# Loading the gate/up levels of the packed half tile once for both of its jobs, and one job earlier in the DMA queue for the jobs that follow

## The chip, the cores and the metric

The kernel runs on one NeuronCore of a Trainium2 chip. Its engines are TensorE (PE; its weight loads are PEld), VectorE (DVE), ScalarE (ACT), GpSimd (POOL) and SyncE (SP), which here only issues DMAs. The metric is device time in microseconds (us) of one execution. Before the change it is 1940.79 us, the median of 3 runs (1940.75 to 1940.89).

## The reference

One layer of a transformer-like tower on 16 x 128 tokens of 1024 features: a generated convolution kernel (the part called tok), then attention, then a gated feed-forward part with quantised weights. The change is in the feed-forward part:

```python
def _qlinear(x, q, scale, A, Bm):
    w = (q.astype(jnp.float32) - Q_ZERO) * (scale * Q_STEP)[:, None]
    y = jnp.einsum('bsh,oh->bso', x, w)
    return y + LR_SCALE * (x @ A @ Bm)
g = _qlinear(x, gate_q, gate_scale, gate_A, gate_B)     # q: (2752, 1024) integers 0..15
u = _qlinear(x, up_q, up_scale, up_A, up_B)
h = jax.nn.silu(g) * u
return _qlinear(h, down_q, down_scale, down_A, down_B)  # q: (1024, 2752)
```

Here x has 2048 rows of 1024 features, and 2752 is 21 tiles of 128 hidden features and a rest of 64.

## The kernel before, in words

**Jobs.** The gate and up products are done in 44 jobs. A job (i, p) is one tile i of hidden features for one half p of the tokens (two chunks, a and b, of 512 tokens each). The order is the list `JOBS`: jobs 0 and 1 are tiles 0 and 1 for the first half of the tokens, computed directly ("whole"). Jobs 2 and 3 are the packed half tile (i = 21) for the first and for the second half of the tokens: the 64 gate rows and the 64 up rows that are left over stand together in one tile of 128, so each of the two jobs has one product per chunk ("half"). Jobs 4 to 43 do tiles 2 to 20 for the first half of the tokens (jobs 4 to 22) and tiles 0 to 20 for the second (jobs 23 to 43), each with seven half-size products in place of eight ("seven"), in the manner of Strassen. Constants: `SEVENS` = 4 is the first of these, `SECOND` = 23 the first of the second half, `NJ` = 44, `FULL` = 21.

**What a job needs.** SP loads the job's integer levels into the one buffer `qraw` (q_raw in the trace: 1024 KB, 512 KB for the half tile), ACT converts them to 16-bit floats in `q16[g % 2]` (q_f in the trace; `convert`, L1671 to L1676), and for a job of seven products POOL forms four sums of them in `qsum[g % 2]` (q_sums; `level_sums`, L1097 to L1106). PE's first product of such a job uses q_f, the second uses q_sums. The semaphore `s_q` counts conversions. As `qraw` is one buffer, `load_rows` waits for the conversion of the load before:

```python
            sp.wait_ge(s_q, g)
```

**Behind the products.** DVE gathers the products of a job into gate and up, ACT applies silu and rounds the hidden values to 16 bits (`high_hidden`), POOL makes their rest (`low_hidden`, L1111, counted by `s_hlo`), and SP stores both (L1021, hidden_parts). PE adds the job's share of the low-rank product of down two jobs later (`inner_product`, L1404), after `s_hlo`. The semaphores of PE's steps on ACT's copies of the low-rank terms of gate and up (`s_term`) keep PE from writing ps_l before ACT has read it: job 4's first matmuls (L1386) wait for job 3's last such copy (`term_half`, first_up, L1716).

**The queue of SP** is written out by hand and every wait in it holds what stands behind it. At place g of its loop it does, in this order: `load_rows(g + 2)`; at g = 23 a load for down's low-rank part; from g = 23 on the load of one tile of down's integer levels (`load_levels`, L991, down_raw, 512 KB), and of two such tiles at g = 23 + 6, 23 + 12 and 23 + 18 (the tuple `TWICE`); the store of job g's hidden values, after `s_hlo`. down_raw is one buffer too, so `load_levels(i)` waits until POOL has converted tile i - 1 (`s_lev`).

**The loop of POOL** at place g: `low_hidden` of job g - 1, `level_sums(g + 1)`, and from g = 24 on the conversion of one tile of down's levels (`convert_levels`, L1115), of two tiles at g = 29, 35 and 41. There are 22 such tiles, 0 to 21: at place 29 POOL converts tiles 5 and 6. SP loads tile 5 at its place 28, and tiles 6 and 7 at its place 29.

**The loop of ACT** at place g: from g = 4 on it copies a low-rank term, applies silu and copies the first product, rounds the hidden values of job g - 1, and then does `convert(g + 1)`. For the jobs up to 4 it does `convert(g + 1)` at the start of the place.

**After the jobs**, down's products (L1511) run on PE.

Of the kernel before, what the change touches and what calls it, by code (L numbers as in the profile page):

```python
# [12 lines left out]
ACT = mybir.ActivationFunctionType  # L13
X = mybir.AxisListType.X

P = 128
# [518 lines left out]
KH = KT // 2  # L535
JOBS = [(0, 0), (1, 0), (FULL, 0), (FULL, 1)] + [(i, 0) for i in range(2, FULL)] + [(i, 1) for i in range(FULL)]
KINDS = ["half" if i == FULL else "whole" if g < 2 else "seven" for g, (i, _) in enumerate(JOBS)]
SEVENS = 4
SECOND = SEVENS + FULL - 2
TWICE = (6, 12, 18)  # L540
NJ = len(JOBS)


class Events:
# [18 lines left out]
PROD = Events(("a", "b"), ("gate_a", "up_a", "gate_b", "up_b"), ("p1", "p6", "p5", "p2", "p7", "p3", "p4"))  # L563
# [119 lines left out]
def layer(nc, t, out, first, rooms, small, xn_hi, xn_lo, ident, mask, h0_dram):  # L683
# [12 lines left out]
    two, four = range(2), range(4)  # L696
    w, wv, raw, raw_v, bias = first.w, first.wv, first.raw, first.raw_v, first.bias
# [43 lines left out]
    qraw = put("q_raw", [P, 2, D], I32, "w")  # L741
    q16 = [put(f"q_f16{s}", [P, 2, D], F16, "w", 8192 + 4096 * s) for s in two]
    qsum = [put(f"q_sums{s}", [P, 4, KH * P], F16, "v0", 8192 + 4096 * s) for s in two]
    hid = [put(f"hidden{s}", [P, BPP, 2, H], F16, "v0", 4096 * s) for s in two]
    q_zero = small("q_zero", [P, 1])
# [29 lines left out]
    with ExitStack() as st:  # L775
# [18 lines left out]
    s_qraw, s_q, s_qsum, s_lraw, s_lev = (sem("g_" + n) for n in ("qraw", "q", "qsum", "lraw", "lev"))  # L794
    s_prod, s_low, s_term, s_first, s_read, s_silu, s_hid, s_hhi, s_hlo, s_inner = (
        sem("g_" + n) for n in ("prod", "low", "term", "first", "read", "silu", "hid", "hhi", "hlo", "inner"))
# [42 lines left out]
    def _(sp):  # L839
# [133 lines left out]
                spread_low(n // 4 - 1)  # L973
        def load_rows(g):
            i = JOBS[g][0]
            sp.wait_ge(s_q, g)
            if i < FULL:
                sp.dma_start(qraw[:], t["gu_q"][i, :, :, :]).then_inc(s_qraw, 16)
            else:
                sp.dma_start(qraw[:, 0, :], t["gu_q"][i, :, 0, :]).then_inc(s_qraw, 16)  # L980
# [11 lines left out]

        level = 0
        for g, (i, p) in enumerate(JOBS):
            if 0 < g < NJ - 2:
                load_rows(g + 2)
            if g == SECOND:
                sp.wait_ge(s_prod, PROD.end(SECOND - 1))
                for done in (s_t1l, s_t3l, s_e2):
                    sp.wait_ge(done, 2 * KH)  # L1000
                sp.dma_start(bd_raw[:], t["down_b"]).then_inc(s_bdraw, 16)
            if g >= SECOND:
                for _ in range(2 if g - SECOND in TWICE else 1):
                    if level < IT:
                        load_levels(level)
                        level += 1
            if g == SECOND + 6:
                sp.wait_ge(s_bd, 1)
                sp.wait_ge(s_t2l, 2 * KH)
                for k in two:  # L1010
                    sp.wait_ge(s_out[k], 16 * (SECOND // 2 + (1 - k) * (SECOND % 2)))
                load_parts(0)
            sp.wait_ge(s_hlo, 2 * g + 2)
            rows = slice(p * BPP, (p + 1) * BPP)
            if i < FULL:
                dst = hid_dram[rows, :, i * 2 * P:(i + 1) * 2 * P].rearrange("n p f -> p n f")
                src = hid[g % 2][:].rearrange("p n a t -> p n (a t)")
            else:
                dst = hid_dram[rows, :, i * 2 * P:HB].rearrange("n p f -> p n f")
                src = hid[g % 2][:, :, 0, :]  # L1020
            sp.dma_start(dst, src).then_inc(s_out[g % 2], 16)  # L1021
# [25 lines left out]
    def _(pool):  # L1047
# [48 lines left out]

        def level_sums(g):  # L1097

            gate1, gate2, up1, up2 = (q16[g % 2][:, m, at * KH * P:(at + 1) * KH * P] for m in two for at in two)
            sum1, sum2, sum3, sum4 = (qsum[g % 2][:, k, :] for k in four)  # L1100
            pool.wait_ge(s_q, g + 1)
            pool.wait_ge(s_prod, PROD.end(g - 2))
            chain.after(tt(sum1, up1, up2, ALU.add))
            chain.after(tt(sum2, sum1, gate1, ALU.subtract))
            chain.mark(tt(sum3, gate1, up1, ALU.subtract))
            tt(sum4, gate2, sum2, ALU.subtract).then_inc(s_qsum, 1)  # L1106
# [23 lines left out]
        for g in range(NJ):  # L1130
# [9 lines left out]
            if SEVENS <= g < SEVENS + 4 * KH:  # L1140
                p, k = sum_at(g)
# [20 lines left out]
    def _(pe):  # L1162
# [202 lines left out]
        def all_features(g, m, bank, p, c):  # L1365

            free(g, bank)
            for k in range(KT):
                lev = q16[g % 2][:, m, k * P:(k + 1) * P]
                nc.tensor.matmul(banks[bank], lev, x2_hi[:, k, chunk(p, c)], start=(k == 0), stop=False)  # L1370
                last = nc.tensor.matmul(banks[bank], lev, x2_lo[:, k, chunk(p, c)], start=False, stop=(k == KT - 1))
            last.then_inc(s_prod, 1)
# [52 lines left out]
        pe.wait_ge(s_term, TERM(0, "up_a"))  # L1425
        low(0, 1, 1, 1)
        for g in (1,):
            pe.wait_ge(s_q, g + 1)
            all_features(g, 0, 0, 0, 0)
            pe.wait_ge(s_term, TERM(g - 1, "gate_b"))  # L1430
            low(g, 0, 0, 0)
            all_features(g, 1, 1, 0, 0)
            pe.wait_ge(s_term, TERM(g - 1, "up_b"))
            low(g, 1, 0, 1)
            all_features(g, 0, 2, 0, 1)
            pe.wait_ge(s_term, TERM(g, "gate_a"))
            low(g, 0, 1, 0)
            all_features(g, 1, 3, 0, 1)
            pe.wait_ge(s_term, TERM(g, "up_a"))
            low(g, 1, 1, 1)  # L1440
        for g in (2, 3):
            p = JOBS[g][1]
            pe.wait_ge(s_q, g + 1)
            all_features(g, 0, 0, p, 0)
            for c in two:
                pe.wait_ge(s_lst[2 * p + c], 16 * 16)
            pe.wait_ge(s_term, TERM(g - 1, "gate_b" if g == 2 else "a"))
            low_half(g, 0)
            inner_product(g - 2)
            all_features(g, 0, 2, p, 1)  # L1450
            pe.wait_ge(s_term, TERM(g - 1, "up_b" if g == 2 else "b"))
            low_half(g, 1)
        for g in range(SEVENS, NJ):
            p = JOBS[g][1]
            a, b, side = chunk(p, 0), chunk(p, 1), 1 + 2 * (g % 2)
            q, sums, fresh = q16[g % 2], qsum[g % 2], g in (SEVENS, SECOND)
            one, two_ = slice(0, KH), slice(KH, KT)
            left, right = slice(0, KH * P), slice(KH * P, D)
            pe.wait_ge(s_q, g + 1)
            if g == SEVENS:  # L1460
                pe.wait_ge(s_term, TERM(g - 1, "b"))
            else:
                pe.wait_ge(s_read, READ(g - 1, "w2"))
            low(g, 0, 0, 0)
            low(g, 0, 1, 1)
            free(g, 0)
            half_features(0, q[:, 0, left], x2_hi[:, one, a], x2_lo[:, one, a], False)
            inner_product(g - 2)
            pe.wait_ge(s_qsum, g - SEVENS + 1)
            if fresh:  # L1470
                pe.wait_ge(s_t2l, KH * (p + 1))
            free(g, side)
            half_features(side, sums[:, 1, :], x2_hi[:, one, b], x2_lo[:, one, b], False)
            pe.wait_ge(s_term, TERM(g, "gate_a"))
            low(g, 1, 1, 0)
            if fresh:
                pe.wait_ge(s_t1l, KH * (p + 1))
            free(g, 2)
            half_features(2, sums[:, 0, :], t1[p][0], t1[p][1], False)
            pe.wait_ge(s_first, SNAP(g, "up"))  # L1480
            half_features(0, q[:, 0, right], x2_hi[:, two_, a], x2_lo[:, two_, a], True)
            pe.wait_ge(s_read, READ(g, "w1"))
            low(g, 1, 0, 1)
            if fresh:
                pe.wait_ge(s_t3l, KH * (p + 1))
            pe.wait_ge(s_read, READ(g, "v"))
            half_features(side, sums[:, 2, :], t3[p][0], t3[p][1], True)
            pe.wait_ge(s_read, READ(g, "x5"))
            half_features(2, sums[:, 3, :], x2_hi[:, two_, b], x2_lo[:, two_, b], True)
            if fresh:  # L1490
                pe.wait_ge(s_t4l, KH * (p + 1))
            pe.wait_ge(s_read, READ(g, "x7"))
            half_features(side, q[:, 1, right], t4[p][0], t4[p][1], True)
# [48 lines left out]
    def _(act):  # L1542
# [126 lines left out]
            nc.scalar.activation(bst[:, m, :], b_raw[:], ACT.Copy, scale=ups[:, 1 + m:2 + m]).then_inc(s_bhi, 1)  # L1669

        def convert(g):  # L1671
            act.wait_ge(s_qraw, 16 * (g + 1))
            if g >= 2:
                act.wait_ge(s_prod, PROD.end(g - 2))
            m = slice(0, 2 if JOBS[g][0] < FULL else 1)
            nc.scalar.activation(q16[g % 2][:, m, :], qraw[:, m, :], ACT.Identity, bias=q_zero[:]).then_inc(s_q, 1)  # L1676

        deviation(0)
        high_features(0)
# [86 lines left out]
            high_sum(0, k, e1[0][k][:], t1[0][0][:, k, :], s_t1h, s_e1)  # L1766
        for g in range(NJ):
            kind = KINDS[g]
            if 2 <= g + 1 <= SEVENS:
                convert(g + 1)  # L1770
            if g == SEVENS - 1:
                act.wait_ge(s_prod, PROD.end(2))
                for k in range(KH):
# [16 lines left out]
            if g:  # L1790
                high_hidden(g - 1, 1)
                high_hidden(g - 1, 0)
            if SEVENS < g + 1 < NJ:
                convert(g + 1)
            if kind == "whole":
                term(g, 0, 1, 0)
# [579 lines left out]
```

## Time and profile before

| | before |
|---|---|
| time, median of 3 | 1940.79 us |
| the profiled execution: its time | 1940.61 us |
| its span (first to last instruction) | 1938.8 us |
| PE busy | 1813.0 us, 94% of the span |
| DVE busy | 1201.4 us, 62% |
| POOL busy | 860.2 us, 44% |
| ACT busy | 714.1 us, 37% |
| mean granted TensorE clock | 0.989 of full speed |
| mean DMA traffic | 101 GB/s |

The jobs run from about 1023 us to about 1630 us of the span, down's products after that. Busy is the share of time in which an engine has an instruction under way. The rows in the section below are of two kinds: in a timeline row the columns are start in us, duration in us (of several merged instructions together where it ends in x2, x3, ...), engine, source line, operation, output and inputs, and in brackets the idle time of the engine just before and what ended it.

### The profile page before, as it was taken

The page shows a single profiled execution, that of the slowest core. Times are in us where ns is not written, and L with a number is a line of the kernel's source. Part 1 is how long each engine was busy: PE and PEld are TensorE (multiplying, and loading weights), DVE is VectorE, ACT ScalarE, POOL GpSimd, SP SyncE. Part 2 cuts the span into 40 slices and gives each one's busy share as a digit, 9 for nine tenths or more (in the row PEclk, how much of TensorE's full clock was granted, in tenths as well). Part 3 has the DMA queues.
Part 4 walks back from the last instruction along what each step waited for, and adds up shares of the span by engine and source line. Part 5 has one row for each costly group of instructions (what it writes and reads, how often), then busy time and mean ns, then how long its engine had stood idle before and what let it go on. Part 6 is the DMA issues. An engine that isn't in the chain of part 4 may idle for free.

```text
span 1938.8 us, 31415 instructions
## 1 busy us (share of the span) xinstructions
PE 1813.0 (94%) x12892; PEld 990.2 (51%) x12892; DVE 1201.4 (62%) x1570; ACT 714.1 (37%) x1027; POOL 860.2 (44%) x593
## 2 busy tenths in 40 slices
PE   0586999999999999999999899999999999999999
PEld 0586665656666656545554344444444444444444
DVE  8996577787878888855657677775755554111111
ACT  4478243343433344422114454453544443000000
POOL 6973134343333334432361576665677774010111
PEclk9988999999999999999999899999999999999999
DMA  2122211111112211144531333434455544434341
GB/s 97 44 66 67 62 56 22 34 39 41 52 53 78 80 60 61 66 158 167 165 104 55 120 109 120 130 99 141 142 181 177 171 155 153 153 102 153 107 148 44
DMA packets 102847, 195.44 MB, mean 101 GB/s; under 512 B 14320, under 2 KB 75504, under 8 KB 92208
## 3 DMA queue, kind: packets, MB, share of 16 engines
q1 hardware_dynamic: 102704, 193.43, 31.2%
q8 instruction: 103, 1.69, 0.4%
q14 instruction: 40, 0.33, 0.1%
HBM read 136.24 MB, written 56.11 MB: 99 GB/s over the span
## 4 chain that ended last, share of the span: by engine, by line
PE 75%; DVE 9%; POOL 2%; issue 2%; ACT 2%; DMA 1%; DVEq 0%; SPq 0%; ACTq 0%
PE acc L1511 15%; PE acc L1377 12%; PE acc L1379 12%; PE ps_p L1169 4%; PE ps_p L1171 4%; PE ps_p L1170 4%; PE acc L1283 3%; PE acc L1285 3%; PE acc L1284 3%; PE ps_t L1196 3%; PE ps_p L1185 2%; PE ps_p L1186 2%; PE ps_p L1187 2%; PE ps_l L1386 2%; POOL prob L1058 1%
## 5 line engine op out<-in xcount | busy, mean ns | idle before, releaser
L1058 POOL TENSOR_TENSOR prob<-prob,mx 128x1024 f32<-128x1024 f32 x64 | 121.4, 1896 | 371.0 <-DVE mx L1878 371.0
L1169 PE MATMUL ps_p<-x_hi,w_qk 128*128 128x512 f16 x512 | 194.7, 380 | 0.0
L1170 PE MATMUL ps_p<-x_lo,w_qk 128*128 128x512 f16 x512 | 194.0, 379 | 0.0
L1171 PE MATMUL ps_p<-x_hi,w_qk 128*128 128x512 f16 x512 | 194.0, 379 | 0.0
L2265 DVE TENSOR_TENSOR y<-acc,down_scale 128x1024 f32<-128x1024 f32 (+1 forms) x17 | 19.8, 1162 | 252.8 <-PE acc L1511 252.8
L1111 POOL TENSOR_TENSOR hidden<-up,hidden 128x512 f16<-128x512 f32 x80 | 91.1, 1160 | 143.0 <-ACT hidden L1737 142.8
L1159 POOL TENSOR_TENSOR lr_term<-lr_term,h_again 128x1024 f32<-128x1024 f32 x16 | 37.6, 2348 | 253.6 <-ACT lr_term L1825 253.6
L1185 PE MATMUL ps_p<-w_v,x_hi 128*128 128x256 f16 x512 | 140.7, 275 | 3.7 <-PEq L805 3.6
L1063 POOL TENSOR_TENSOR prob<-prob,sm 128x1024 f32<-128x1024 f32 x64 | 120.1, 1896 | 52.9 <-DVE sm L1885 52.9
L1186 PE MATMUL ps_p<-w_v,x_hi 128*128 128x256 f16 x512 | 140.7, 275 | 0.0
L1187 PE MATMUL ps_p<-w_v,x_lo 128*128 128x256 f16 x512 | 140.6, 275 | 0.0
L1571 ACT ACTIVATE pth<-ps_t 128x512 f16<-128x512 f32 x128 | 76.1, 595 | 163.8 <-PE ps_t L1196 163.7
L258 PE MATMUL ssm_ps<-phase,magnitude 128*128 128x128 f32 x512 | 70.7, 298 | 64.9 <-DVE magnitude L469 61.7
L2130 DVE SCALAR_TENSOR_TENSOR up<-acc,gu_scale,up 128x512 f32<-128x512 f32 x120 | 90.0, 750 | 61.1 <-PE acc L1379 60.0
L2130 DVE SCALAR_TENSOR_TENSOR gate<-acc,gu_scale,gate 128x512 f32<-128x512 f32 x120 | 89.7, 748 | 56.1 <-PE acc L1379 55.3
L1377 PE MATMUL acc<-x_hi,q_f 128*128 128x512 f16 x320 | 122.3, 382 | 0.0
L1379 PE MATMUL acc<-x_lo,q_f 128*128 128x512 f16 x320 | 122.2, 382 | 0.0
L1377 PE MATMUL acc<-x_hi,q_sums 128*128 128x512 f16 x320 | 121.7, 380 | 0.0
L1379 PE MATMUL acc<-x_lo,q_sums 128*128 128x512 f16 x320 | 121.3, 379 | 0.0
L1377 PE MATMUL acc<-x_sum,q_sums 128*128 128x512 f16 x320 | 121.3, 379 | 0.0
L1379 PE MATMUL acc<-x_sum,q_sums 128*128 128x512 f16 x320 | 121.3, 379 | 0.0
L1889 DVE SCALAR_TENSOR_TENSOR ptl<-ps_t,pth 128x512 f16<-128x512 f32 x128 | 87.7, 685 | 47.2 <-ACT pth L1571 46.8
(343 smaller groups left out, 4382.6 us busy)
## 6 DMA issues: line engine op xcount, KB each, us to landing
q_raw<-in_gu_q SPq DMA_DIRECT2D x42, 1024.0 KB, 6.2
hid_parts<-hidden_parts SPq DMA_DIRECT2D x16, 1376.0 KB, 6.6
hidden_parts<-hidden SPq DMA_DIRECT2D x42, 512.0 KB, 3.5
down_raw<-in_down_q SPq DMA_DIRECT2D x22, 512.0 KB, 3.7
w_raw<-in_w_qk SPq DMA_DIRECT2D x8, 1024.0 KB, 4.9
h_tokens<-n_tok SPq DMA_DIRECT2D x16, 512.0 KB, 3.7
o_parts<-ot SPq DMA_DIRECT2D x32, 256.0 KB, 2.3
wv_raw<-in_w_o SPq DMA_DIRECT2D x8, 1024.0 KB, 4.8
```

Source lines behind the costliest of these rows:

```text
L1058: nc.gpsimd.tensor_tensor(prob[s % 2][p][:], prob[s % 2][p][:], bc(mx[p][:], H, 2), ALU.subtract).then_inc(s_sub[p], 1)
L1063: nc.gpsimd.tensor_tensor(prob[s % 2][p][:], prob[s % 2][p][:], bc(sm[p][:], H, 2), ALU.mult).then_inc(s_prob[p], 1)
L1169: nc.tensor.matmul(out[:], w[:, j % 2, m, 0, at], xn_hi[:, k, tok], start=(k == 0), stop=False)
L1170: nc.tensor.matmul(out[:], w[:, j % 2, m, 0, at], xn_lo[:, k, tok], start=False, stop=False)
L1171: last = nc.tensor.matmul(out[:], w[:, j % 2, m, 1, at], xn_hi[:, k, tok], start=False, stop=(k == KT - 1))
L1185: nc.tensor.matmul(out, xn_hi[:, k, tok], wv[:, g % 2, 0, at], start=(k == 0), stop=False)
L1186: nc.tensor.matmul(out, xn_hi[:, k, tok], wv[:, g % 2, 1, at], start=False, stop=False)
L1187: last = nc.tensor.matmul(out, xn_lo[:, k, tok], wv[:, g % 2, 0, at], start=False, stop=(k == KT - 1))
L1377: nc.tensor.matmul(banks[bank], lev[:, k * P:(k + 1) * P], hi[:, k, :], start=(k == 0 and not adds), stop=False, skip_group_check=adds)
L1379: last = nc.tensor.matmul(banks[bank], lev[:, k * P:(k + 1) * P], lo[:, k, :], start=False, stop=(k == KH - 1), skip_group_check=adds)
L1511: last = nc.tensor.matmul(acc[n % 2][:, b, :], parts[n % 3][:, at], levels[i][:, b * CH:(b + 1) * CH], start=(i == 0 and part == 0), stop= ...
L2130: stt(to[:], banks[bank], scl[:, m, i:i + 1], to[:], ALU.mult, ALU.add).then_inc(s_read, 1)
```

## The change

The two jobs of the packed half tile use the same levels. They are now loaded once and converted once, into one of the two buffers q_f, and both jobs read them there. `LOADS[g]` gives the number of the load whose levels job g uses (0, 1, 2, 2, 3, 4, ..., 42), and takes the place of g in the choice of the buffer and in the counts waited for. The loads of jobs 4 and later are issued one place earlier in SP's loop: `load_rows(4)` and `load_rows(5)` at places 0 and 1, `load_rows(g + 3)` at places 3 to 40. ACT converts job 4's levels where it converted job 3's.

```diff
+LOADS = [g if g < SEVENS - 1 else g - 1 for g in range(NJ)]
...
         def load_rows(g):
             i = JOBS[g][0]
-            sp.wait_ge(s_q, g)
+            sp.wait_ge(s_q, LOADS[g])
...
         for g, (i, p) in enumerate(JOBS):
-            if 0 < g < NJ - 2:
-                load_rows(g + 2)
+            if g < 2:
+                load_rows(g + SEVENS)
+            if 2 < g < NJ - 3:
+                load_rows(g + 3)
...
         def level_sums(g):
-            gate1, gate2, up1, up2 = (q16[g % 2][:, m, at * KH * P:(at + 1) * KH * P] for m in two for at in two)
+            gate1, gate2, up1, up2 = (q16[LOADS[g] % 2][:, m, at * KH * P:(at + 1) * KH * P] for m in two for at in two)
...
-            pool.wait_ge(s_q, g + 1)
+            pool.wait_ge(s_q, LOADS[g] + 1)
...
         def convert(g):
-            act.wait_ge(s_qraw, 16 * (g + 1))
+            act.wait_ge(s_qraw, 16 * (LOADS[g] + 1))
             if g >= 2:
-                act.wait_ge(s_prod, PROD.end(g - 2))
+                act.wait_ge(s_prod, PROD.end(1 if g == SEVENS else g - 2))
             m = slice(0, 2 if JOBS[g][0] < FULL else 1)
-            nc.scalar.activation(q16[g % 2][:, m, :], qraw[:, m, :], ACT.Identity, bias=q_zero[:]).then_inc(s_q, 1)
+            nc.scalar.activation(q16[LOADS[g] % 2][:, m, :], qraw[:, m, :], ACT.Identity, bias=q_zero[:]).then_inc(s_q, 1)
...
-            if 2 <= g + 1 <= SEVENS:
-                convert(g + 1)
+            if g == 1:
+                convert(2)
+            if g == 2:
+                convert(SEVENS)
```

PE's waits on `s_q` and its choice of q16 change in the same way, to `LOADS[g] + 1` and `LOADS[g] % 2`.

**SP where the half tile's jobs are.** Before, the rows of SP's queue from the store of job 0 on (hidden0 and hidden1 are the buffers of hidden values; a row of 128x1024 into q_raw is the half tile; the wait is named by its semaphore, g_q being `s_q` and g_hlo `s_hlo`):

```order
L1021 DMA hidden_parts<-hidden0_1975 128x8x256 [waits g_hlo]
L980 DMA q_raw_1970<-in_gu_q 128x1024 [waits g_q]
L1021 DMA hidden_parts<-hidden1_1976 128x8x256 [waits g_hlo]
L978 DMA q_raw_1970<-in_gu_q 128x2048 [waits g_q]
L1021 DMA hidden_parts<-hidden0_1975 128x8x128 [waits g_hlo]
```

The same stretch now:

```order
L979 DMA q_raw_1970<-in_gu_q 128x2048 [waits g_q]
L1024 DMA hidden_parts<-hidden0_1975 128x8x256 [waits g_hlo]
L979 DMA q_raw_1970<-in_gu_q 128x2048 [waits g_q]
L1024 DMA hidden_parts<-hidden1_1976 128x8x256 [waits g_hlo]
L1024 DMA hidden_parts<-hidden0_1975 128x8x128 [waits g_hlo]
```

The second load of the half tile is gone, job 4's load stands before the store of job 0 (it stood behind the store of job 1), and job 5's before the store of job 1.

**ACT where job 4's levels are converted.** Before (q_f160 and q_f161 are the two buffers of converted levels; x_hi and sum belong to the operands of the seven products):

```order
L1676 ACTIVATE q_f161_1972<-q_raw_1970,q_zero_1977 128x1024
L1716 ACTIVATE first_gate_1964<-ps_l,g_half_back_1952 128x512
L1729 ACTIVATE gate11_1959<-gate11_1959 128x512
L1737 ACTIVATE hidden1_1976<-up11_1963 128x4x128
L1737 ACTIVATE hidden1_1976<-up10_1962 128x4x128
L1716 ACTIVATE first_up_1965<-ps_l,g_half_back_1952 128x512
L1729 ACTIVATE gate00_1956<-gate00_1956 64x512
L1676 ACTIVATE q_f160_1971<-q_raw_1970,q_zero_1977 128x2048
L1744 ACTIVATE x_hi_64<-sum200_2006 128x512
```

And now:

```order
L1679 ACTIVATE q_f161_1972<-q_raw_1970,q_zero_1977 128x2048
L1719 ACTIVATE first_gate_1964<-ps_l,g_half_back_1952 128x512
L1732 ACTIVATE gate11_1959<-gate11_1959 128x512
L1740 ACTIVATE hidden1_1976<-up11_1963 128x4x128
L1740 ACTIVATE hidden1_1976<-up10_1962 128x4x128
L1719 ACTIVATE first_up_1965<-ps_l,g_half_back_1952 128x512
L1732 ACTIVATE gate00_1956<-gate00_1956 64x512
L1747 ACTIVATE x_hi_64<-sum200_2006 128x512
```

The full conversion stands where the half one stood, and the place where it stood is closed up.

**SP where down's levels are loaded twice** (places 28 and 29). Before, from the store of job 27 on:

```order
L1021 DMA hidden_parts<-hidden1_1976 128x8x256 [waits g_hlo]
L978 DMA q_raw_1970<-in_gu_q 128x2048 [waits g_q]
L991 DMA down_raw_2023<-in_down_q 128x1024 [waits g_lev]
L1021 DMA hidden_parts<-hidden0_1975 128x8x256 [waits g_hlo]
L978 DMA q_raw_1970<-in_gu_q 128x2048 [waits g_q]
L991 DMA down_raw_2023<-in_down_q 128x1024 [waits g_lev] x2
```

And now:

```order
L1024 DMA hidden_parts<-hidden1_1976 128x8x256 [waits g_hlo]
L979 DMA q_raw_1970<-in_gu_q 128x2048 [waits g_q]
L992 DMA down_raw_2023<-in_down_q 128x1024 [waits g_lev]
L1024 DMA hidden_parts<-hidden0_1975 128x8x256 [waits g_hlo]
L979 DMA q_raw_1970<-in_gu_q 128x2048 [waits g_q]
L992 DMA down_raw_2023<-in_down_q 128x1024 [waits g_lev] x2
```

The rows read alike; what differs is the job whose levels are loaded and the count that the load waits for. At place 29 it was job 31's load, behind the conversion of job 30's levels; it is job 32's load, behind the conversion of job 31's.

## Rows read from the trace of the kernel before

**Rows 1.** Windows: us, busy us of each engine, clock, DMA share, GB/s

```profile
1152.00:1330.00 178.00, 178.00 (x839) 77.58 (x838) 123.91 (x162) 85.67 (x117) 119.15 (x101) 1.00 0.37 116
```

**Rows 2.** Waits from 1000 to 1130 us: total us, times, longest us

```profile
PE ps_l L1386 <- ACT first_up L1716: 8.9, 1, 8.9
...
ACT q_f L1676 <- DMA q_raw<-in_gu_q: 7.7, 1, 7.7
```

**Rows 3.** Timeline of SP's queue around the half tile's jobs

```profile
1048.60 1.24 SPq L949 DMA_DIRECT2D low_stack<-low_lo  x2
...
1067.06 0.58 SPq L978 DMA_DIRECT2D q_raw<-in_gu_q  x1
```

**Rows 4.** Timeline of ACT, same stretch

```profile
1060.30 1.13 ACT L1676 ACTIVATE q_f<-q_raw,q_zero 128x1024 f16<-128x1024 int32 x1
...
1073.28 2.00 ACT L1676 ACTIVATE q_f<-q_raw,q_zero 128x2048 f16<-128x2048 int32 x1 [7.67 <-DMA q_raw<-in_gu_q]
...
1077.83 0.61 ACT L1729 ACTIVATE gate<-gate 64x512 f32<-64x512 f32 x1
...
1081.79 0.67 ACT L1716 ACTIVATE first_up<-ps_l,g_half_back 128x512 f32<-128x512 f32 x1
```

**Rows 5.** Timeline of PE, jobs 3 and 4

```profile
1068.98 0.41 PE L1391 MATMUL ps_l<-low_stack,gu_b_stack 128*64 128x512 f16 x2
...
1073.31 0.41 PE L1391 MATMUL ps_l<-low_stack,gu_b_stack 128*64 128x512 f16 x2
1082.60 1.01 PE L1386 MATMUL ps_l<-low_stack,gu_b_stack 128*128 128x512 f16 x2 [8.88 <-ACT first_up L1716]
...
1087.25 0.39 PE L1377 MATMUL acc<-x_hi,q_sums 128*128 128x512 f16 x1
...
1096.65 0.38 PE L1377 MATMUL acc<-x_sum,q_f 128*128 128x512 f16 x1 [0.17 <-DVE up L2130]
```

**Rows 6.** Timeline of DVE, same stretch

```profile
1062.56 1.30 DVE L2136 TENSOR_TENSOR up<-gate,up 128x512 f32<-128x512 f32 x2 [2.03 <-ACT gate L1729]
...
1078.48 2.74 DVE L2136 TENSOR_TENSOR up<-gate,up 64x512 f32<-64x512 f32 x2 [10.30 <-ACT gate L1729]
...
1087.44 0.76 DVE L2113 SCALAR_TENSOR_TENSOR up<-acc,g_half_scl,first_up 64x512 f32<-64x512 f32 x1
```

**Rows 7.** A window of PE's wait, columns as in Rows 1

```profile
1077.00:1078.00 1.00, 0.00 (x0) 0.00 (x0) 0.00 (x0) 1.00 (x3) 0.92 (x2) 0.50 0.00 0
```

**Rows 8.** Timeline of ACT: conversions of levels of jobs 30 and 31

```profile
1429.33 2.00 ACT L1676 ACTIVATE q_f<-q_raw,q_zero 128x2048 f16<-128x2048 int32 x1
...
1442.93 2.00 ACT L1676 ACTIVATE q_f<-q_raw,q_zero 128x2048 f16<-128x2048 int32 x1
```

**Rows 9.** Timeline of SP's queue, place 29

```profile
1431.79 0.58 SPq L978 DMA_DIRECT2D q_raw<-in_gu_q  x1
1439.02 6.89 SPq L991 DMA_DIRECT2D down_raw<-in_down_q  x2
```

**Rows 10.** Timeline of POOL: level tile 6, last sum for job 31

```profile
1442.78 2.77 POOL L1115 TENSOR_SCALAR x_hi<-down_raw 128x1024 f16<-128x1024 int32 x1 [3.79 <-DMA down_raw<-in_down_q]
...
1451.44 1.15 POOL L1106 TENSOR_TENSOR q_sums<-q_f,q_sums 128x512 f16<-128x512 f16 x1
```

**Rows 11.** Timeline of PE: start of job 31, its second product

```profile
1451.99 0.59 PE L1386 MATMUL ps_l<-low_stack,gu_b_stack 128*128 128x512 f16 x2
...
1454.80 0.39 PE L1377 MATMUL acc<-x_hi,q_sums 128*128 128x512 f16 x1
```

**Rows 12.** Source line L991: the 22 loads of down's levels

```profile
DMA to landing us min/median/max: 3.4/3.7/7.4
```

**Rows 13.** Source line L978: the 40 full loads of gate/up levels

```profile
DMA to landing us min/median/max: 4.8/6.2/9.9
```

**Rows 14.** Timeline of POOL: level tiles 13 and 20

```profile
1524.36 2.77 POOL L1115 TENSOR_SCALAR x_lo<-down_raw 128x1024 f16<-128x1024 int32 x1 [3.72 <-DMA down_raw<-in_down_q]
...
1606.67 2.77 POOL L1115 TENSOR_SCALAR down_levels<-down_raw 128x1024 f16<-128x1024 int32 x1 [4.39 <-DMA down_raw<-in_down_q]
```

More of the change, by code:

```diff
@@ L1368, in all_features @@
             for k in range(KT):
-                lev = q16[g % 2][:, m, k * P:(k + 1) * P]
+                lev = q16[LOADS[g] % 2][:, m, k * P:(k + 1) * P]
                 nc.tensor.matmul(banks[bank], lev, x2_hi[:, k, chunk(p, c)], start=(k == 0), stop=False)
@@ L1427, in _ @@
         for g in (1,):
-            pe.wait_ge(s_q, g + 1)
+            pe.wait_ge(s_q, LOADS[g] + 1)
             all_features(g, 0, 0, 0, 0)
@@ L1442, in _ @@
             p = JOBS[g][1]
-            pe.wait_ge(s_q, g + 1)
+            pe.wait_ge(s_q, LOADS[g] + 1)
             all_features(g, 0, 0, p, 0)
@@ L1455, in _ @@
             a, b, side = chunk(p, 0), chunk(p, 1), 1 + 2 * (g % 2)
-            q, sums, fresh = q16[g % 2], qsum[g % 2], g in (SEVENS, SECOND)
+            q, sums, fresh = q16[LOADS[g] % 2], qsum[g % 2], g in (SEVENS, SECOND)
             one, two_ = slice(0, KH), slice(KH, KT)
             left, right = slice(0, KH * P), slice(KH * P, D)
-            pe.wait_ge(s_q, g + 1)
+            pe.wait_ge(s_q, LOADS[g] + 1)
             if g == SEVENS:
@@ L1792, in _ @@
                 high_hidden(g - 1, 0)
-            if SEVENS < g + 1 < NJ:
+            if SEVENS <= g < NJ - 1:
                 convert(g + 1)
```

## The prediction

> **What bounds the kernel now.** I read the windows first, then the waits, then the timelines around the longest wait of TensorE, and last the timelines further on of every queue that the change touches. In the jobs of seven products PE is busy for all of 178 us, at full clock, while every other engine has spare time [rows 1]: what is added elsewhere costs nothing there until it makes PE wait. The largest wait of PE in the feed-forward part is one of 8.9 us, and ACT waits 7.7 us for a load of levels [rows 2]. The timelines join the two. SP has issued its last low_stack copies by 1048.60 + 1.24 = 1049.84 us, but job 4's load goes out only at 1067.06 [rows 3]. ACT has it at 1073.28 after 7.67 us of idling, converts for 2.00 us, and only then reaches first_up at 1081.79, on which PE has been waiting since the end of job 3 [rows 4, 5]. The wait has a second price, the clock: in the middle of it the granted clock is 0.50, the 1.2 GHz level, against 1.00, the 2.4 GHz level, in the steady jobs [rows 1, 7]. From the start of job 4 to its second product PE takes 1087.25 - 1082.60 = 4.65 us, and 1454.80 - 1451.99 = 2.81 us for the same piece of job 31 at full clock [rows 5, 11].
>
> **The change, part by part: the early gain.** Job 4's load is issued behind the low_stack copies, at 1049.9 us, since the conversion that it waits for is long done. With the usual 6.2 us to landing it is there at 1056.1, with the longest, 9.9, at 1059.8 [rows 13]: both ahead of ACT's turn at 1060.30. That conversion is now the full one, 2.00 for 1.13 us [rows 4], and it pushes what follows it on ACT, and through it DVE and PE in job 3, by 0.87 us. The half conversion of job 3 and one 512 KB load go; their time lay in the waits. PE then ends job 3 at 1073.31 + 0.41 + 0.87 = 1074.59 [rows 5]. ACT's other work need not be late: its copy of job 3's first term can start at 1068.98 + 0.41 + 0.87 = 1070.26, the silu some 0.67 us later, at 1070.9, and DVE's product 0.65 us behind that (1077.83 to 1078.48), at 1071.55 [rows 4 to 6]; the rounding of job 2's hidden values follows within 2 us. So what is late next is PE's own last matmul of job 3: first_up starts at 1074.6 and job 4 0.81 us behind it (1081.79 to 1082.60), at 1075.4. That is 7.2 us early, with an idle time of 0.8 us that I take as too short to cost clock. By its second product PE would be 1087.25 - (1075.4 + 2.81) = 9.0 us early. But at the end of job 4 PE waits for DVE even now, 0.17 us [rows 5], so it cannot gain more than DVE does. DVE's chain runs without a pause from 1078.48 to the L2113 at 1087.44; its first two products took 2.74 us there and 1.30 at 1062.56 [rows 6]. From 1071.55, with 1.30 for 2.74, it reaches L2113 at 1079.07 instead of 1087.44: 8.4 us early. I take -8.4. The bounds: -7.0, if the slow pair of DVE's products comes again (1.44 us), and -9.0, PE's own figure. POOL's sums for job 4 start earlier, within its idle time.
>
> **The part that costs: SP's waits further on.** From place 3 on, each `load_rows` stands at the same spot in the queue, but loads a job further, and so waits for one conversion more. qraw is one buffer, so that wait is needed. Conversions come every 13.6 us [rows 8]; the load at place g used to find its conversion done, and now waits nearly a whole job for it, with everything behind it. Behind it stand the store of hidden values and, from place 23, down's levels.
>
> The stores first. Before, the store of job g is released by POOL's low_hidden; the conversion of job g + 2's levels ends at about the same time, so the store is later by one issue, 0.6 us. Its readers (the buffer's next use two jobs later) are 20 us off: nothing.
>
> The single level tiles: a tile that was issued some 7 us behind low_hidden is now issued 0.6 us behind the end T of the next conversion. POOL must wait for it until T + 6.6; its 2.77 us end at T + 9.4, and low_hidden is due again some 2.3 us (an estimate) before the next conversion ends, at T + 11.3. That fits, also with a landing of 7.4 us (T + 10.8). Nothing.
>
> The double tiles at places 29 and 35 do not fit. POOL there converts tile 5, and then tile 6, which SP issues in its place 29. Now it is issued at 1439.02, as soon as POOL has freed the buffer; the 6.89 us of the row are the distance to the second of the two [rows 9]. POOL gets it at 1442.78 after a wait of 3.79 us, and then needs until 1451.44 + 1.15 = 1452.59 for the tile, low_hidden and the sums of job 31: 9.81 us [rows 10]. PE takes these sums at 1454.80 [rows 11], so the slack is 2.2 us. After the change the load in front of tile 6 waits for the conversion of job 31's levels, which ends at 1442.93 + 2.00 = 1444.93 [rows 8]. It takes 0.58 us to issue, so tile 6 goes out at 1445.55, behind 1024 KB. No row shows a level tile right behind such a load alone. Bounds: 3.8 us from issue to POOL's start, as now, and 7.4, the longest of the 22 [rows 12]. A 1024 KB load with a 512 KB store just in front takes 6.2 [rows 13], and a tile behind 1024 KB waits for the same 1536 KB; I take 6.0. POOL starts at 1451.55, the sums are done at 1461.4, and PE, which has nothing else to do, stands still for 6.6 us (4.3 to 8.0 by the bounds). At the end of the long wait of today the clock was at the lower level, and the restart cost 4.65 - 2.81 = 1.8 us. I take this again, since the stall is of that kind; bounds 0 and twice it, 3.6. Place 35 has the same distances [rows 14], where POOL waits 3.72 us for tile 13 as it waits 3.79 us for tile 6 at place 29. Two stalls: 2 x (6.6 + 1.8) = 16.8 us.
>
> Two sentences bear on this, and no number above needs them. The Trainium skill, page "DMA: Bandwidth & Descriptors", section "Anatomy of one DMA — SWDGE (gpsimd) path", says that DMA engines do not wait on semaphores, the wait is done by the issuing sequencer before dispatch. By that rule tile 6 cannot pass the load ahead of it, and the rival of no stall is excluded; the trace agrees in that SP issues nothing between 1431.79 and 1439.02. The same section of the Trainium skill fits a DMA with a fixed 2.0 us plus its bytes at 436 GB/s, for another way of issuing; the estimate by it for 1.5 MB is 5.6 us from the load's issue, 5.0 from the tile's, and the sum would be 2 us lower.
>
> The double tile at place 41 has no `load_rows` in front (they end at place 40), only tile 19 is late. The conversion at place 40 ends at 1442.93 + 2.00 + 11 x 13.6 = 1594.5; tile 19 is issued at 1595.1, there at 1601.1, converted at 1603.9; tile 20 follows 4.4 us later (POOL's wait of today) [rows 14], at 1608.3, and the sums end at 1618.1, where PE wants them at 1454.80 + 12 x 13.6 = 1618.0. So +0.1, up to 1.5 us with a landing of 7.4.
>
> **The sum.** -8.4 + 16.8 + 0.1 = +8.5 us. The profiled execution took 1940.6 us (span 1938.8 and 1.8 around it), the median of the runs is 1940.8, 0.2 more. So 1940.8 + 8.5 = 1949.3 us, 0.4% slower. Of this kernel a measurement tells about 0.2%, 3.9 us, from no change.
>
> **The rivals.**
> - *No stall, faster.* The early gain is real, and down's levels are never waited for. It decides itself at places 29 and 35: POOL would have to start on tile 6 by 1444.8 us (slack 2.2 us behind 1442.78). Against it: the issue alone is at 1445.55. For it: only that I may have the counts of the wait or the order of the queue wrong. Time: 1940.8 - 8.4 = 1932.4 us.
> - *Short stalls, no change.* The tile lands as fast as it does now, and the clock does not fall, since low_hidden done at mid-stall lets PE do its small inner product and cuts the idle time in two. 2 x 4.3 - 8.4 = +0.2: 1941.0 us. For it: most level tiles take 3.7 us; against it: 1024 KB are in front.
> - *Longer stalls.* The tile takes 9.9 us, as the slowest load of levels did [rows 13], behind the stores and loads that now bunch up: 2 x (10.5 + 1.8) - 8.4 + 1.5 = +17.7: 1958.5 us.
>
> **How the numbers follow.** Forecast 0.80, no stall 0.10, short stalls 0.06, longer stalls 0.04. The forecast's own range, from -9.0 with stalls of 4.3 and little clock to -7.0 with 8.0 and a bit over 1.8, is about 1943 to 1956; it, and short stalls at its edge, hold somewhat over 8 in 10, and the range stops there, with the fast case left out. Of the forecast's 0.80 I put 0.01 below 1944.7. Faster 0.10, within 0.2% 0.07, slower 0.83.
>
> **What the profile after would show.** Job 4's conversion at about 1060.3 us with no wait for its DMA, and job 4's first matmul at about 1075.4; PE then some 8.4 us early up to job 30. Then two waits of PE for q_sums of POOL in jobs 31 and 37, each of 4 to 8 us (in part before the inner product), with a clock of 0.5 at its end, and POOL waiting some 11 us for down_raw at places 29 and 35 where it waited 3.8. I am wrong if SP issues tile 6 before the conversion of job 31 ends, if PE shows no wait after 1400 us, or if its wait before job 4 is not shorter than 3 us. Wrong in size only, if the tile's landing or the clock's share differ.

## The result, and the profile after

| | before | after |
|---|---|---|
| time, median of 4 runs each | 1940.77 us | 1955.39 us |
| lowest and highest | 1939.27, 1940.89 | 1954.16, 1957.09 |
| the profiled execution: its time, its span | 1940.61, 1938.8 us | 1956.57, 1954.8 us |
| mean granted TensorE clock | 0.989 | 0.985 |

The changed kernel is slower: 1.0078 of the time before, 95% interval 1.006 to 1.0095. The forecast was 1949.3 us, within 1943 to 1956. The direction was right, and so was the mechanism of the stalls; of the +14.6 us the forecast had +8.5, and most of what is missing lies in its early gain.

The waits of PE over 0.8 us between 1000 and 1660 us of the changed kernel (total us, times, longest us):

```profile
PE acc L1380 <- POOL q_sums L1109: 9.7, 2, 4.8
PE ps_i L1407 <- POOL hidden L1114: 3.8, 2, 1.9
PE acc L1373 <- DVE up L2118: 3.4, 1, 3.4
PE ps_l L1389 <- ACT first_up L1719: 0.9, 1, 0.9
```

The wait of 8.9 us of [rows 2] has become 0.9 (last row). Two waits of 4.8 us for POOL's sums are new, each with one of 1.9 in front of it, and a wait that was 1.5 us before is now 3.4 (third row); of that one the forecast has only 0.87 us, for the longer conversion, and nothing for the clock.

SP's queue in the changed kernel, around the half tile's jobs and at place 29, which answer to [rows 3, 9]:

```profile
1052.84 0.58 SPq L979 DMA_DIRECT2D q_raw<-in_gu_q  x1
1056.04 0.38 SPq L1024 DMA_DIRECT2D hidden_parts<-hidden  x1
1065.27 0.34 SPq L979 DMA_DIRECT2D q_raw<-in_gu_q  x1
...
1443.30 0.33 SPq L979 DMA_DIRECT2D q_raw<-in_gu_q  x1
1443.67 8.84 SPq L992 DMA_DIRECT2D down_raw<-in_down_q  x2
```

Job 4's load goes out at 1052.84 instead of 1067.06, although this execution was 2.97 us late by then (see the table below). The load in front of tile 6 waits for the conversion of job 31's levels, 1441.28 + 2.00 = 1443.28 on ACT, and leaves 0.02 us later; tile 6 follows at 1443.67. ACT's conversion for job 4, which answers to [rows 4], has lost its wait of 7.67 us for the load:

```profile
1063.26 1.99 ACT L1679 ACTIVATE q_f<-q_raw,q_zero 128x2048 f16<-128x2048 int32 x1
```

What POOL and PE make of tile 6, timelines of the changed kernel that answer to [rows 10, 11]:

```profile
1449.38 2.77 POOL L1118 TENSOR_SCALAR x_hi<-down_raw 128x1024 f16<-128x1024 int32 x1 [9.88 <-DMA down_raw<-in_down_q]
...
1458.36 1.60 POOL L1109 TENSOR_TENSOR q_sums<-q_f,q_sums 128x512 f16<-128x512 f16 x1
```

```profile
1450.33 0.59 PE L1389 MATMUL ps_l<-low_stack,gu_b_stack 128*128 128x512 f16 x2
...
1454.55 0.62 PE L1407 MATMUL ps_i<-hidden,down_a 128*64 128x512 f16 x4 [1.89 <-POOL hidden L1114]
...
1460.01 0.61 PE L1380 MATMUL acc<-x_hi,q_sums 128*128 128x512 f16 x1 [4.84 <-POOL q_sums L1109]
...
1466.20 0.38 PE L1380 MATMUL acc<-x_hi,q_f 128*128 128x512 f16 x1
```

POOL waits 9.88 us for tile 6 where it waited 3.79; its last sum ends at 1459.96, and PE's second product starts at 1460.01. Undisturbed it would start 2.81 us behind 1450.33, at 1453.14: PE stands still for 6.87 us. The lower clock adds to it. Windows of the changed kernel (columns as in [rows 1]):

```profile
1459.00:1460.00 1.00, 0.00 (x0) 0.00 (x0) 0.61 (x1) 1.00 (x2) 0.95 (x1) 0.50 0.96 289
...
1464.00:1465.00 1.00, 1.00 (x4) 0.30 (x2) 1.00 (x2) 0.00 (x0) 1.00 (x2) 0.50 1.02 434
...
1466.00:1467.00 1.00, 1.00 (x6) 0.47 (x5) 0.60 (x1) 0.00 (x0) 0.92 (x2) 1.00 0.75 288
```

The granted clock is at the 1.2 GHz level at the end of PE's stall and for some 5 us more of work, and back at 2.4 GHz by 1466.

**Where the time is, piece by piece.** PE's timeline gives the start of each job (its first pair of low-rank matmuls, L1386 before, L1389 after). The table compares the profiled execution of every kernel with that of before. "Start" is where the pair in job 1 begins, 1039.82 us before; "early" is the time from there to the start of job 5, 58.56 us before (42.78 to job 4, and job 4's 15.78); then jobs 31 and 37, 13.61 us each before. Everything is in us, as the difference to before. The kernels e1 to e6 are those of the experiments below.

| kernel | start | early | job 31 | job 37 | sum | its time less 1940.61 |
|---|---|---|---|---|---|---|
| after | +2.97 | -4.63 | +9.38 | +8.26 | +15.98 | +15.96 |
| e1_levels_first | -2.17 | -4.58 | 0 | 0 | -6.75 | -6.76 |
| e2_one_double_fewer | -0.03 | -5.86 | 0 | +8.92 | +3.03 | +3.01 |
| e3_before_tile_held | -0.95 | -0.08 | +7.36 | +7.20 | +13.53 | +13.55 |
| e4_sums_held | +0.66 | -3.47 | +8.65 | +9.63 | +15.47 | +15.46 |
| e5_late_conversion | +0.18 | -8.03 | 0 | 0 | -7.85 | -7.89 |
| e6_two_loads_early | +1.42 | -5.88 | 0 | 0 | -4.46 | -4.48 |

The last two columns agree within 0.04 us in every kernel, so nothing else moved. The column "start" is not the edit's: none of the kernels changes an instruction ahead of that point. In the changed kernel the difference arises in the first 160 us. This is the window of 0 to 160 us, before and then after:

```profile
0.00:160.00 160.00, 80.63 (x618) 78.94 (x619) 142.69 (x153) 94.87 (x170) 122.52 (x107) 0.95 0.21 66
```

```profile
0.00:160.00 160.00, 78.57 (x591) 76.71 (x592) 145.81 (x150) 92.19 (x165) 118.08 (x105) 0.94 0.21 66
```

PE shows 27 matmuls fewer by then; from 160 to 1000 us its busy time is 808.59 us before and 808.53 after. The start differs by up to 5 us between executions. Without it the change costs -4.63 + 9.38 + 8.26 = +13.0 us in the profiled executions.

### The profile page after: what moved, and what is told of

It is laid out like the page before. It is cut to its first block, busy times and chain, and to the rows that moved or that the text cites. A ratio compares the mean times of both kernels' runs of the same rounds, so it can differ in the third digit from the quotient of the medians.

```text
span 1954.8 us, 31412 instructions
## 1 busy us (share of the span) xinstructions
PE 1819.0 (93%) x12892; PEld 992.3 (51%) x12892; DVE 1211.4 (62%) x1570; ACT 713.4 (36%) x1026; POOL 860.3 (44%) x593
## 4 chain that ended last, share of the span: by engine, by line
PE 72%; DVE 9%; POOL 3%; issue 3%; ACT 2%; DMA 1%; SPq 0%; DVEq 0%; ACTq 0%; POOLq 0%
PE acc L1514 15%; PE acc L1380 11%; PE acc L1382 11%; PE ps_p L1172 4%; PE ps_p L1174 4%; PE ps_p L1173 4%; PE acc L1286 3%; PE acc L1288 3%; PE acc L1287 3%; PE ps_t L1199 3%; PE ps_p L1188 2%; PE ps_p L1189 2%; PE ps_p L1190 2%; PE ps_l L1389 2%; POOL prob L1061 1%
```

## The experiments

The theory: the stalls of jobs 31 and 37 come from one thing, tile 6 (and 13) standing behind a load that waits for a conversion; and nearly half of the early gain was lost because POOL's sums for job 4 ran beside DVE's products. A rival for the first is that the bunched traffic itself slows the tiles; for the second, that the fall of the clock has nothing to do with POOL. The first rival did not hold up; for the second e4 and e5 speak.

**e1_levels_first.** From place 23 on the level tiles go ahead of the load in SP's queue.

```diff
-            if 2 < g < NJ - 3:
+            if 2 < g < SECOND:
                 load_rows(g + 3)
...
                         load_levels(level)
                         level += 1
+            if SECOND <= g < NJ - 3:
+                load_rows(g + 3)
```

> After, but from place 23 on SP issues down's level tiles of a place before the load of gate/up levels of that place. My theory (the wait in front of the tile in SP's queue makes the two stalls): tile 6 goes out as soon as POOL has freed its buffer, jobs 31 and 37 take 13.6 us each again instead of 23.0 and 21.9, and the time is that of before less the early gain of 4.6 us, 1936 us. The rival (the tile is late because more DMA traffic now bunches up around it): it lands late from wherever it is issued, POOL still waits over 6 us for it, and at least half of the 17.6 us stays, 1945 us or more.

Measured: 1933.95 us (median of 6; before on the same chip 1940.39), 0.9967 of before, interval 0.9954 to 0.998. SP's queue and POOL at place 29, timelines of e1_levels_first:

```profile
1432.28 6.84 SPq L992 DMA_DIRECT2D down_raw<-in_down_q  x2
1439.16 0.43 SPq L979 DMA_DIRECT2D q_raw<-in_gu_q  x1
```

```profile
1435.99 2.77 POOL L1120 TENSOR_SCALAR x_hi<-down_raw 128x1024 f16<-128x1024 int32 x1 [3.74 <-DMA down_raw<-in_down_q]
```

POOL's wait is the 3.7 us of before, both jobs are back at 13.61, and PE has no wait for q_sums. The waits of PE that are left here:

```profile
PE acc L1375 <- DVE up L2120: 3.4, 1, 3.4
PE ps_l L1391 <- ACT first_up L1721: 0.9, 1, 0.9
```

The order in the queue is the whole loss of jobs 31 and 37, and the early gain is as small as in the changed kernel.

**e2_one_double_fewer.** The changed kernel with `TWICE = (12, 18)` for `(6, 12, 18)`: place 29 converts one tile.

> After, with double level tiles at places 35 and 41 only (21 tiles are converted by place 43, and the 22nd as well: 20 places and two doubles). My theory: each double tile with a load in front makes one stall, so job 31 takes 13.6 us and only job 37 about 22 us; 9.4 us less than after, 1946 us in a run like its median. The rival (the stalls belong to these two jobs, by buffers or counts of conversions, not to the double tiles): both jobs stay long, 1955 us.

Measured: 1943.62 us (one run). Only job 37 is long, and PE waits for the sums once:

```profile
PE acc L1380 <- POOL q_sums L1109: 4.8, 1, 4.8
```

So the stall needs the double tile: a single one fits behind the late load, as the prediction has it. The time is 2.4 us under the expected 1946, in part by the early column (-5.86 for -4.63), which is explained further on.

**e3_before_tile_held.** The kernel before, with the wait alone and no load ahead of the tile:

```diff
             if g >= SECOND:
                 for _ in range(2 if g - SECOND in TWICE else 1):
                     if level < IT:
+                        if g - SECOND in (6, 12):
+                            sp.wait_ge(s_q, g + 3)
                         load_levels(level)
```

> Before, with one wait added: at places 29 and 35 SP waits for the conversion of the levels of job g + 2 before it issues the level tiles. Loads, conversions and buffers are as before. My theory: the wait alone makes the stalls. As no 1024 KB load is right in front, the tile is there 3.8 us after its issue, so PE stands for 4 to 5 us in jobs 31 and 37, and with 2 to 3 us of clock each job is 6 to 8 us longer: 1953 to 1956 us. If only the load in front of the tile (traffic) were the cause, the stalls would be under 2 us each, 1941 to 1945 us.

Measured: 1954.16 us (one run). Timelines of SP and POOL at place 29 in e3_before_tile_held:

```profile
1443.93 6.87 SPq L991 DMA_DIRECT2D down_raw<-in_down_q  x2
```

```profile
1447.68 2.77 POOL L1117 TENSOR_SCALAR x_hi<-down_raw 128x1024 f16<-128x1024 int32 x1 [9.72 <-DMA down_raw<-in_down_q]
```

The wait by itself costs 7.2 to 7.4 us a job. The tile, with nothing in front, is there 1447.68 - 1443.93 = 3.75 us after its issue; in the changed kernel it takes 1449.38 - 1443.67 = 5.71. The 1024 KB in front account for 2.0 us of the landing, and jobs 31 and 37 are 2.0 and 1.1 us longer with them (9.38 and 8.26 for 7.36 and 7.20); the traffic is the smaller part.

**e4_sums_held.** The changed kernel, POOL's sums for job 4 held until DVE's products of job 2 are done:

```diff
         def level_sums(g):
+            if g == SEVENS:
+                pool.wait_ge(s_hid, 2 * g - 2)
```

> After, with POOL's sums for job 4 held until DVE has made job 2's hidden products (a wait added to POOL, nothing else). My theory of the missing 3.8 us of early gain: these sums run at the same time as DVE's products of job 1 (2.25 for 1.30 us), which makes PE's wait before job 3 3.4 us long instead of 2.4, and in it the clock falls. Expected: DVE's pair back at 1.3 us, that wait 2.4 us, granted clock 1.0 in job 3, job 4 starts 3 to 4 us earlier against job 1; about 1951.5 us. The rival (the longer conversion on ACT alone is to blame): the wait and the clock in job 3 stay as they are, 1955 us.

Measured: 1956.07 us (one run), where 1951.5 was expected and 1955 by the rival. The half of the theory that concerns DVE is confirmed, the half that concerns the clock is not. DVE in the changed kernel, then in e4_sums_held:

```profile
1066.37 2.25 DVE L2141 TENSOR_TENSOR up<-gate,up 128x512 f32<-128x512 f32 x2 [2.88 <-ACT gate L1732]
...
1070.09 2.87 DVE L2148 TENSOR_TENSOR hidden<-up,hidden 128x512 f16<-128x512 f32 x2
```

```profile
1064.06 1.29 DVE L2143 TENSOR_TENSOR up<-gate,up 128x512 f32<-128x512 f32 x2 [2.88 <-ACT gate L1734]
...
1076.56 3.06 DVE L2152 TENSOR_TENSOR hidden<-up,hidden 64x512 f16<-64x512 f32 x2
1079.66 3.33 DVE L2164 TENSOR_TENSOR x_lo<-sum,x_hi 128x512 f16<-128x512 f32 x4
```

With POOL idle the first pair takes 1.29 us again, as before the change [rows 6], and PE waits 2.40 us instead of 3.36 for what follows it: the 1.55 us of before and the 0.87 us of the longer conversion, which is still there. But the clock still falls (timeline and window of e4_sums_held, the window's columns as in [rows 1]):

```profile
1066.94 0.59 PE L1375 MATMUL acc<-x_hi,q_f 128*128 128x512 f16 x1 [2.40 <-DVE up L2120]
...
1072.00 0.41 PE L1396 MATMUL ps_l<-low_stack,gu_b_stack 128*64 128x512 f16 x2
...
1083.09 0.38 PE L1382 MATMUL acc<-x_hi,q_sums 128*128 128x512 f16 x1 [2.83 <-issue]
```

```profile
1068.00:1069.00 1.00, 1.00 (x3) 0.29 (x2) 0.94 (x3) 1.00 (x3) 0.00 (x0) 0.50 0.00 0
```

The window shows 0.50, and job 3's first product takes 1072.00 - 1066.94 = 5.06 us where it took 3.54 before (1065.44 to 1068.98). So the clock is lost without POOL's sums too: the wait that the longer conversion leaves is enough for it. The sums, now late, ran beside DVE's next work instead (last two rows of the second DVE fence: 3.06 us for 1.29, and 3.33 us for the 2.50 that the same four operations take in the changed kernel). These x_lo are operands of job 4's second product, which waited 2.83 us and started 0.10 us behind them (1079.66 + 3.33 = 1082.99): job 4 took 17.96 us instead of 14.52.

**e5_late_conversion.** e1_levels_first, with ACT's conversion for job 4 moved from the start of its place 2 to behind its last silu there:

```diff
             if g == 2:
-                convert(SEVENS)
...
             gate(g, 0)
+            if g == 2:
+                convert(SEVENS)
```

> The kernel of e1, with job 4's conversion on ACT moved from the start of place 2 to its end, behind the silu of job 2's first chunk. Nothing full stands in front of the copies that DVE and PE wait for in jobs 2 and 3, and POOL's sums start after DVE's products of job 1. My theory (the longer conversion and POOL's sums beside DVE's products lengthen PE's wait before job 3, and this wait costs clock): PE's wait before job 3 falls from 3.4 to under 1 us, the clock stays at 1.0, the stretch from job 1's second pair of low-rank matmuls to job 4 takes 35 to 36 us instead of 39.4, and the time is 3 to 4 us less than that of e1, about 1930.5 us. The rival (the early part is bound by something else, such as the order of DVE's own work): the stretch stays at 39 us.

Measured: 1932.72 us (median of 5; before on that chip 1941.91), 0.9959 of before, interval 0.9945 to 0.9973. The timeline of PE in e5_late_conversion:

```profile
1065.36 0.38 PE L1375 MATMUL acc<-x_hi,q_f 128*128 128x512 f16 x1 [1.31 <-DVE up L2120]
...
1068.91 0.41 PE L1396 MATMUL ps_l<-low_stack,gu_b_stack 128*64 128x512 f16 x2
```

The wait is 1.31 us (expected: under 1), the clock stays up (granted 1.00 in every microsecond from 1064 to 1081), and job 3's first product takes 3.55 us. The early column gains 3.45 us over e1, as expected; job 4 gives 1.25 back, since the sums now run beside the next pair of DVE's (second row). The first row is the pair ahead of job 3:

```profile
1061.68 2.09 DVE L2143 TENSOR_TENSOR up<-gate,up 128x512 f32<-128x512 f32 x2 [0.99 <-ACT gate L1734]
...
1070.62 2.75 DVE L2143 TENSOR_TENSOR up<-gate,up 64x512 f32<-64x512 f32 x2 [2.52 <-ACT gate L1734]
```

That pair is still slow, 2.09 us, beside earlier operations of POOL's (x_sum). So what keeps PE's wait short here, and the clock up, is that the conversion no longer stands ahead of the pair, and not that POOL keeps still.

The two intervals, of e1 and of e5, overlap: that e5 beats e1 rests on the pieces of one profile each, not on the times, which differ by 1.2 us with a start that scatters by more.

**e6_two_loads_early.** The changed kernel, with each load from place 4 on back where it was (`if 3 < g < NJ - 2: load_rows(g + 2)`), so that only the loads of jobs 4 and 5 come early.

> After, but only the loads of jobs 4 and 5 are early; from job 6 on the load of job g + 2 stands at place g, as in before. My theory: the early gain comes from the first two places alone and the stalls from the later ones, so jobs 31 and 37 take 13.6 us and the stretch before job 4 about 39 us, 1934 to 1937 us. A rival (without the earlier loads the conversions of the later jobs come too late with two buffers whose roles are swapped): some job of 5 to 43 grows by over 0.5 us.

Measured: 1936.13 us (one run); jobs 31 and 37 take 13.61, and no job from 5 to 43 grew, against the rival. The early gain needs only the first loads; to have the later ones a job sooner earns nothing and makes the stalls. The timeline of PE around job 3's first product in e6_two_loads_early:

```profile
1068.66 0.59 PE L1373 MATMUL acc<-x_hi,q_f 128*128 128x512 f16 x1 [3.36 <-DVE up L2118]
...
1073.80 0.41 PE L1394 MATMUL ps_l<-low_stack,gu_b_stack 128*64 128x512 f16 x2
```

The code up to here is that of the changed kernel and so is the wait, but the product takes 5.14 us.

## Why the prediction was right, and where its sizes were off

**The stalls: right.** Forecast 2 x (6.6 + 1.8) = 16.8 us, measured 9.38 + 8.26 = 17.64. The chain came link by link: conversion, load, tile 6 0.4 us behind it, POOL's start 5.7 us after the issue (forecast 6.0), the sums, PE 6.87 us late (forecast 6.6). PE stands for 6.90 us in job 37, so the clock's part is 9.38 - 6.87 = 2.5 us in job 31 and 8.26 - 6.90 = 1.4 in job 37, for the forecast's 1.8. Part of POOL's lateness is its own: from tile 6 to the last sum it took 10.58 us for 9.81, as its last two sums took 1.48 and 1.60 us for 1.16 and 1.15, beside DVE; this outweighs the landing (5.7 for 6.0) and the shorter way from the conversion to tile 6's issue (0.39 for 0.62). All 22 level tiles now land in 3.5/6.5/7.1 us (min/median/max) where they took 3.4/3.7/7.4 [rows 12]; the choice of 6.0, by the combined bytes and not by the median of 3.7, was the nearer one. Even with the 3.75 us of e3 the stall would still be 7.3 us a job. The rival of short stalls failed on two counts: the tile took 5.7 us, and the clock fell although PE did its inner product in the middle of the stall. The sign named for POOL, a wait of some 11 us, measured 9.88; the forecast's own times give 1451.55 - (1442.78 - 3.79) = 12.6, but POOL was itself held up before, by 2.26 us for tile 5.

**Place 41: right.** Forecast +0.1, measured 0; jobs 43 to the end take the same 323.5 us in both kernels.

**The early gain: the mis-sized term.** Forecast -8.4, bounds -7.0 to -9.0; measured -4.63, outside them. The load, ACT's conversion without a wait, and the wait of 0.9 us before job 4 came as forecast. Two steps failed, both about PE's wait before job 3. The larger is that the longer conversion "pushes what follows it on ACT, and through it DVE and PE in job 3, by 0.87 us": the longer wait was priced at its length alone, the clock in it at nothing. The smaller is the sentence "POOL's sums for job 4 start earlier, within its idle time". They are within POOL's idle time, but not within DVE's. The timeline of POOL in the changed kernel:

```profile
1066.68 1.38 POOL L1106 TENSOR_TENSOR q_sums<-q_f 128x512 f16<-128x512 f16 x1 [1.27 <-PE acc L1374]
1068.15 1.48 POOL L1107 TENSOR_TENSOR q_sums<-q_sums,q_f 128x512 f16<-128x512 f16 x1
```

The first sum starts 0.31 us into DVE's pair of products of 1066.37, on which PE's next product depends; the pair takes 2.25 us for 1.30 [rows 6]. That is 0.95 us, and e4, with the sums out of the way, takes it back. With the 0.87 us of the longer conversion, which the forecast had, PE's wait before job 3 grows from 1.55 to 3.36. In it the clock falls, which it did not in 1.55. The timeline of PE in the changed kernel, and a window of it (columns as in [rows 1]):

```profile
1070.21 0.59 PE L1373 MATMUL acc<-x_hi,q_f 128*128 128x512 f16 x1 [3.36 <-DVE up L2118]
...
1076.60 0.41 PE L1394 MATMUL ps_l<-low_stack,gu_b_stack 128*64 128x512 f16 x2
...
1082.20 0.59 PE L1389 MATMUL ps_l<-low_stack,gu_b_stack 128*128 128x512 f16 x2 [0.87 <-ACT first_up L1719]
```

```profile
1075.00:1076.00 1.00, 1.00 (x4) 0.31 (x3) 0.00 (x0) 0.00 (x0) 0.00 (x0) 0.50 0.73 215
```

Job 3's first product takes 6.39 us, most of it at the lower clock; in e5, at full clock, 3.55, so 2.84 us are the clock's. 0.95 + 2.84 = 3.79 us, and 8.4 - 4.63 = 3.77 are missing. How much the clock takes differs between executions of the same code with the same wait of 3.36 us: the product took 6.39 and 6.44 us (after, e1) or 5.16 and 5.14 (e2, e6). That is the difference between the early gains of -4.6 and -5.9. The clock's part does not need POOL's sums: it is there in e4 (1.5 us) after a wait of 2.40 us without the sums, and gone in e5 with a slow pair of DVE's but without the conversion ahead of it. Whether POOL's 0.95 us alone, on top of the 1.55, would bring the clock down, no run shows.

The Trainium skill, page "SBUF — State Buffer", section "SBUF: two separate sides", states that GpSimd and VectorE share a pair of SBUF ports as an exclusive lock, held for a whole instruction, and that a VectorE operation with both inputs in SBUF takes it against a GpSimd operation that reads SBUF. The trace agrees within 0.2 us: by that rule the three operations run one after the other, 0.65 + 1.15 + 0.65 = 2.45 us from 1066.37 (an estimate from [rows 6, 10]), and DVE's pair ended after 2.25. That it is the ports and nothing else that the two share, no run here tests.

**The sum.** -4.63 + 17.64 = +13.0 against the forecast's +8.5: 3.8 of the 4.5 us are the early gain, 0.8 the stalls. The rest up to the medians' +14.6 is no more than the start's scatter.

**The forecast's form.** The chance of 0.83 for slower went to the right case. The range held the time by 0.6 us, and partly by luck: its upper end is said to be -7.0 with stalls of 8.0 and "a bit over 1.8" of clock, which with 2.0 gives 1940.8 - 7.0 + 20.0 = 1953.8, under the 1955.39 measured; 1956 needs 3.1 us of clock a stall. Nor was there room for the start that differs between executions: the profile of a single execution doesn't show it, four runs do.

## What to carry to other kernels

Prefetching a step further in a hand-written in-order queue moves the wait of every load behind it; look at each instruction that stands behind such a load, find its consumer with the least slack, and if it has less slack than the wait, put the load behind it (one moved line turned +14.6 us into -6.4). Where a step is made longer ahead of a wait of PE, price the clock as well as the length: 0.87 us more of wait cost 1.5 us more by the clock in e4. And where work is moved into an engine's idle time, look at what the others do in that time (DVE beside POOL here), not at its own timeline alone. If only the first steps were late, move only those.

## What the runs showed of the hardware

- DVE's pairs of tensor_tensor with both inputs in SBUF took 1.28 to 1.30 us beside an idle POOL, and 2.09 to 3.06 us beside its tensor_tensors, at every place to which the experiments moved the sums (2.25 in the changed kernel, 3.06 in e4, 2.75 in e5); POOL's own took up to 1.60 us for 1.15.
- PE's clock was at the lower level after waits of 3.36 and 2.40 us before job 3, and stayed at full speed through 1.55 and 1.31 us in the same place. After the wait of 3.36 us the next product took 5.14, 5.16, 6.39 and 6.44 us in four executions, after 2.40 us 5.06, and 3.55 at full clock.
- POOL could start on a 512 KB load 3.75 us after its issue with no load just ahead of it in the queue (e3), and 5.71 us after it right behind one of 1024 KB.
